# Attention pass of a graph kernel: transposed one-hots made by TensorE transposes and ScalarE copies instead of broadcast target rows

## Chip, cores and metric

One NeuronCore of a Trainium2 (trn2) chip runs one program. The metric is device time in microseconds (us), lower is better. "The time" of a kernel is the median of several runs; next to it stands one profiled execution, from which all rows of the profile come.

## What is computed

Two blocks, each a graph layer followed by a mixture-of-experts layer, on 6250 nodes of 256 features. The change touches the first graph layer alone, a graph attention layer over 206,250 edges that are sorted by target:

```
x = x + L0_gnn(layernorm(x))
h     = (x @ W).reshape(N, 4, 64)
a_src = einsum('nhc,hc->nh', h, att_src);  a_dst = einsum('nhc,hc->nh', h, att_dst)
e     = leaky_relu(a_src[src] + a_dst[dst], 0.2)
p     = exp(e - m[dst]);  denom = segment_sum(p, dst)
out   = segment_sum(p / denom[dst] * h[src], dst) + bias;  relu(out)
...
x = x + L0_ffn(...)    # 8 experts, 2 per node
x = x + L1_gnn(...)    # the same sorted edges, weighted sums, no attention
x = x + L1_ffn(...)    # a second attention over 131,072 unsorted edges, 4 experts
```

## The kernel before, in words

The sorted edges are cut into NS = 1664 tiles of 128 edges such that all targets of a tile lie in one block of 128 nodes. `plan_steps` (L451) makes, once, per tile the source of each edge, its target relative to the block's first node, its weight, and the block's number. `graph_pass` (L612) runs twice: with attention (tag g0, `attend` true; L745, L835, L877 to L901, L932 to L953, L977, L991 are its lines) and without (tag g1; L758, L846, L855, L991). Lines L855 and L991 are shared by both passes.

The tiles go in SG = 208 groups of GRP = 8, and the groups in rounds of RINGS = 4: gathered rows G and one-hots S have four slots, one for each group of a round. Below, "step k" is the work of one group. In the attention pass each engine runs its own instruction queue:

- GpSimd (POOL) issues eight indirect DMAs per group (L745), each fetching 128 source rows of 260 floats into G. Group k may start when all eight sums of group k-4 are done (L742); a small copy (L736) stages the indices first.
- SyncE (SP) issues, per group, one DMA (L723) that broadcasts 1024 relative targets to all 128 partitions, into a slot of ST; it waits until the spread of the group four before has used that slot (L722). The rows come from `target_rows`, a table in DRAM that `plan_steps` writes at L494 after a subtraction (L544).
- ScalarE (ACT) turns the broadcast rows into transposed one-hots in place with two activations over 128x1024: |row - lane| (L932) and relu(1 - that) (L934). It also makes the exponentials (L952, L953), and in the middle 200 groups a side job, a counting sort of the last layer's edges (L938, L942).
- TensorE (PE) first does the second half of the sums of group k-1 (four tiles, L991), then `spread` of group k+1 (L977): eight products of a transposed one-hot with the block's attention terms, which give each edge its target's term; then the first half of the sums of group k. A sum multiplies one-hot S by rows G into one of four PSUM banks (pM); a bank is used again when VectorE has added it (L990).
- VectorE (DVE), per step k: loads eight block numbers into registers (L447), waits for the spread of k (L875) and for the gather (L876), adds (L877, L878), leaky relu (L882), adds bank 0 of group k-1 into the accumulator (L855), subtracts (L888), makes all eight one-hots of group k+1 in one instruction (L835), adds banks 1 to 3, waits for the exponentials, and then alternates four multiplications of G by the factors (L899) with the last four adds.

The side job has three stretches: step 0 to 3 prepares, steps 4 to 103 count, steps 104 to 203 rank. In the rank stretch VectorE also does, every second step, a scan (L812, behind the one-hots) and a predicated copy (L818, at the end of the step).

The one instruction for eight one-hots reads the lane numbers from PSUM (pN, filled at L912):

```
v.tensor_tensor(S[:, r], pN[:, :].unsqueeze(1).broadcast_to([P, GRP, P]),
                REL[:, bass.ds(k * GRP, GRP)].unsqueeze(2).broadcast_to([P, GRP, P]),
                ALU.is_equal).then_inc(s["onehot"], 1)
```

The second pass makes them one at a time from SBUF, in turn with the adds (L846, `step_weighted`, L904). The last layer's slot pass has broadcast rows of its own (`slot_rows`), and is not touched.

Of the kernel before, what the change touches and what calls it, by code (L numbers as in the profile page):

```python
# [33 lines left out]
P = 128  # L34
# [145 lines left out]
def setup(sh, x):  # L180
# [9 lines left out]
    sh.minus_lane = sh.sb("minus_lane", [P, 1])  # L190
    s_x, s_cst, s_pre = sh.sem("x_loaded"), sh.sem("constants"), sh.sem("memsets")
    sh.x_ready = (s_x, 7 * 16)
    with Scope(nc) as sc:
# [3 lines left out]
        def _(pool):  # L197
# [6 lines left out]
            for out, mult in ((sh.lane, 1), (sh.minus_lane, -1)):  # L204
                pool.iota(out[:, :], [[0, 1]], base=0, channel_multiplier=mult,
                          allow_small_or_imprecise_dtypes=True).then_inc(s_cst, 1)
# [244 lines left out]
def plan_steps(sh, first_dst, edges, planned, planned_block, target_rows, stats):  # L451
# [9 lines left out]
                                          "stored", "relative")}  # L461
# [5 lines left out]
    with Scope(nc) as sc:  # L467
# [9 lines left out]
        FIRST = sc.sb("plan_FIRST", [P, SCH])  # L477
        T = sc.sb("plan_T", [P, SCH], I32)
        BI = sc.sb("plan_BI", [P, NS], I32)
# [11 lines left out]
        def _(sp):  # L491
            sp.dma_start(F[:, :], bcast_rows(first_dst[0, :])).then_inc(s["first"], 16)
            sp.wait_ge(s["relative"], NBK)
            sp.dma_start(target_rows.rearrange("(c p) m -> p c m", p=P), RF[:, 1, :, :]).then_inc(s["stored"], 16)  # L494
# [4 lines left out]
            sp.wait_ge(s["stored"], 16 * (NA + 2))  # L499
# [14 lines left out]
        def _(v):  # L514
# [16 lines left out]
            then(v.tensor_scalar(FIRST[:, :], TF[:, :], -1.0, float(P), ALU.add, ALU.mult))  # L531
# [3 lines left out]
            then(v.tensor_scalar(BI[:, :].rearrange("p (a b) -> p a b", a=4), flat, -1.0, None, ALU.add))  # L535
            norm.on_vector(v)
            for bk in range(NBK):
# [3 lines left out]
                for a in range(2):  # L541
                    v.tensor_copy(RF[:, a, c0:c1, :], RAW[:, a, c0:c1, :]).then_inc(s["float"], 1)
                v.wait_ge(s["float"], bk * 2 + 2)
                v.tensor_tensor(RF[:, 1, c0:c1, :], RF[:, 1, c0:c1, :], FIRST[:, c0:c1].unsqueeze(2).broadcast_to([P, c1 - c0, P]),  # L544
                                ALU.subtract).then_inc(s["relative"], 1)
                for a in range(NA):
                    v.wait_ge(s["turned"], bk * NA + a + 1)
                    out = pT[(bk * NA + a) % 2][:, 0:(c1 - c0) * P]
                    if a == 0:
                        v.tensor_copy(OSRC[:, cols], out).then_inc(s["out"], 1)  # L550
                    else:
                        v.tensor_copy(OUT[:, a - 1, cols], out).then_inc(s["out"], 1)
# [4 lines left out]
        def _(pe):  # L557
# [5 lines left out]
            for bk in range(NBK):  # L563
                for a in range(NA):
# [3 lines left out]
                    if a == 0:  # L568
                        pe.wait_ge(s["float"], bk * 2 + 1)
                    elif a == 1:  # L570
                        pe.wait_ge(s["relative"], bk + 1)
# [40 lines left out]
def graph_pass(sh, tag, planned, planned_block, table, width, acc, acc_zeroed, gather_done, rounds0, keep=None, gmax=None,  # L612
               sort=None, target_rows=None, place=0):
# [13 lines left out]
    if attend:  # L627
        names += ["iota", "far", "turned", "ad", "z", "lr", "arg", "p", "pcol", "gp"]
# [3 lines left out]
    s_rows = [sh.sem(f"{tag}_rows{r}") for r in range(RINGS)] if attend else None  # L632
    with Scope(nc) as sc:
# [18 lines left out]
        if attend:  # L652
            ST = sc.sb(f"{tag}_ST", [P, RINGS, GRP, P])
# [3 lines left out]
            pN = sc.ps(f"{tag}_pN", [P, P])  # L657
            pAX = [sc.ps(f"{tag}_pA{j}", [P, 512]) for j in range(2)]
            pA = [x[:, 0:GRP * HEADS].rearrange("p (u h) -> p u h", u=GRP) for x in pAX]
            pF = sc.ps(f"{tag}_pF", [P, 512])  # L660
            before, totals = pAX[0][:, 128:128 + NB + 1], pAX[0][:, 256:256 + NB + 1]
# [47 lines left out]
        def _(sp):  # L709
# [16 lines left out]
            if attend:  # L726
                over_groups(sp, rows)
# [1855 lines left out]
```

## Time and profile before

| what | value |
|---|---|
| time, median of 3 runs | 9814.81 us (9797.74 to 9833.64) |
| the profiled execution | 9757.08 us, span 9755.1 us |
| mean granted TensorE clock | 0.708 of 2.4 GHz |
| attention pass (first gather issue to last sum) | 205 to 3262 us |
| second graph pass | 4834 to 7507 us |

How to read the rows: times are us from the span's start, except means, which are ns. PE is TensorE's matmuls, PEld its weight loads, DVE VectorE, ACT ScalarE, POOL GpSimd, SPq the DMA issues of SyncE. An fp32 matmul stands as two PE records. In a group of instructions, "idle before" is the time that the engine stood idle right before instructions of the group, with what ended it: an instruction of another engine, a DMA, "issue" (nothing that the profile shows was waited for) or "remote" (a semaphore whose setter the profile does not tie to a record).

### The profile page before, as it was taken

Reading aid. Unit: us, or ns where it says so; the run is one execution under the profiler, and the core shown is the slowest. Engines: PE = TensorE matmul, PEld = TensorE weight load, DVE = VectorE, ACT = ScalarE, POOL = GpSimd, SP = SyncE. Lnnn points to the kernel's source line nnn. Section 1 sums busy time; section 2 is a strip of 40 time slices with the busy share of each in tenths; the row PEclk is TensorE's granted clock in tenths of the full one; section 3 lists DMA queues with packets and bytes.
Section 4 is the critical chain, followed back from the end, with each engine's and each line's share of the span. In section 5 each row is a group of like instructions: output and inputs, shape, how many; then the busy total and the mean of one; then the engine's idle time right before and its main releaser. Section 6 shows DMA issues by size and latency. Waiting matters only on the chain. (4 is left out here: it accounts for less than half of the span.)

```text
span 9755.1 us, 110833 instructions
## 1 busy us (share of the span) xinstructions
PE 5735.5 (59%) x25980; PEld 4596.0 (47%) x25981; DVE 3970.9 (41%) x10089; ACT 1833.0 (19%) x3782; POOL 5610.6 (58%) x6058
## 2 busy tenths in 40 slices
PE   3666656555555248888144444444444459898984
PEld 2444444434444247777133322322322348888884
DVE  4555555555555640000444444444443432222225
ACT  1222222222222023333000000000000123333331
POOL 3555555555555546666666666666666346666662
PEclk7666676666666669999566666666666757888886
DMA  3333333333333314444333222222222022222256
GB/s 128 113 116 115 115 116 113 103 99 102 103 103 100 109 56 135 135 135 136 115 88 88 81 81 80 81 81 79 81 81 61 1 56 64 65 66 66 63 63 158
DMA packets 459979, 909.45 MB, mean 93 GB/s; under 512 B 133272, under 2 KB 272908, under 8 KB 459615
## 3 DMA queue, kind: packets, MB, share of 16 engines
q0 software_dynamic: 237808, 481.17, 20.3%
q1 hardware_dynamic: 222062, 427.12, 13.0%
q8 instruction: 33, 0.54, 0.0%
q14 instruction: 76, 0.61, 0.0%
HBM read 836.02 MB, written 71.83 MB: 93 GB/s over the span
## 5 line engine op out<-in xcount | busy, mean ns | idle before, releaser
L991 PE MATMUL g_pM<-g_G,g_S 128*128 128x260 f32 (+1 forms) x6656 | 2555.0, 536 | 2857.8 <-DVE acc L855 1374.7
L991 PEld LDWEIGHTS g_pM<-g_G,g_S 128*128 128x128 f32 x6656 | 1608.6, 262 | 3692.7 <-DVE acc L855 2142.8
L745 POOL DMA_INDIRECT g_G<-table,g_STG x1664 | 1626.3, 977 | 1377.1 <-PE g_pM L991 872.6
L758 POOL DMA_INDIRECT g_G<-table,g_IDX x1664 | 1583.6, 952 | 891.0 <-issue 471.2
L855 DVE TENSOR_TENSOR acc<-g_pM,acc 128x260 f32 (+1 forms) x3328 | 1412.3, 424 | 1356.9 <-remote 588.4
L1551 POOL DMA_INDIRECT q_G<-table,slot x1072 | 1040.1, 970 | 636.3 <-issue 288.3
L607 POOL DMA_INDIRECT slots<-sort_PAIR,sort_ADDR x1024 | 1024.0, 1000 | 523.0 <-issue 310.8
L846 DVE TENSOR_SCALAR g_S<-iota,g_REL,g_WT 128x128 f32<-128x128 f32 x1664 | 596.1, 359 | 454.5 <-issue 274.7
L1337 PE MATMUL q_pH<-ew_XT,ew_W 128*128 (+1 forms) x3136 | 563.2, 352 | 58.3 <-issue 29.4
L977 PEld LDWEIGHTS g_pA<-keep,g_ST 128*128 128x128 f32 x3328 | 520.1, 245 | 119.8 <-issue 118.0
L1211 ACT ACTIVATE f_XT<-f_pT 128x512 f32<-128x512 f32 x49 | 28.9, 597 | 2902.3 <-issue 2736.0
L899 DVE TENSOR_TENSOR g_G<-g_G,g_pF 128x512 f32<-128x512 f32 x832 | 563.3, 677 | 0.0
L1337 PEld LDWEIGHTS q_pH<-ew_XT,ew_W 128*128 128x128 f32 x3136 | 525.1, 259 | 77.3 <-ACT ew_GT L1356 40.2
L2244 PE MATMUL e_pH<-e_XT,e_W 128*128 128x128 f32 x3360 | 447.1, 297 | 168.2 <-ACT e_XT L2188 151.1
L977 PE MATMUL g_pA<-keep,g_ST 128*128 x3328 | 515.6, 287 | 49.5 <-issue 34.5
L2244 PEld LDWEIGHTS e_pH<-e_XT,e_W 128*128 128x128 f32 x3360 | 428.3, 210 | 208.1 <-ACT e_GT L2205 177.8
L877 DVE TENSOR_TENSOR g_Z<-g_G,g_pA 128x32 f32<-128x32 f32 x208 | 39.0, 187 | 1102.4 <-remote 1012.3
L952 ACT ACTIVATE g_pF<-g_ARG 128x32 f32<-128x32 f32 x208 | 41.8, 201 | 2283.3 <-DVE g_ARG L888 1974.3
L2222 DVE TENSOR_TENSOR e_Y<-e_pY,ew_B 128x256 f32<-128x256 f32 x105 | 44.6, 425 | 986.6 <-PE e_pY L2252 882.6
L1347 PE MATMUL q_pY<-ew_W,ew_GT 128*128 128x256 f32 x1568 | 440.1, 430 | 2.8 <-issue 2.6
L2252 PE MATMUL e_pY<-ew_W,e_GT 128*128 x1680 | 389.2, 384 | 8.9 <-issue 7.7
L2205 ACT ACTIVATE e_GT<-e_pH,ew_VT 128x128 f32<-128x128 f32 x840 | 239.6, 369 | 693.8 <-remote 407.2
(319 smaller groups left out, 6384.0 us busy)
## 6 DMA issues: line engine op xcount, KB each, us to landing
e_W<-in_L_ffn_W SPq DMA_DIRECT2D x210, 512.0 KB
g_ST<-target_rows SPq DMA_DIRECT2D x208, 512.0 KB
sort_PAIR<-slot_rows SPq DMA_DIRECT2D x66, 512.0 KB
g_G<-table,g_STG POOLq DMA_INDIRECT x1664
g_G<-table,g_IDX POOLq DMA_INDIRECT x1664
ys_all<-ew_Y SPq DMA_DIRECT2D x196, 128.0 KB
sm_Y<-ys_all SPq DMA_DIRECT2D x28, 896.0 KB, 10.3
q_ST<-slot_rows SPq DMA_DIRECT2D x34, 512.0 KB
```

The source lines that it names most:

```text
L607: pool.indirect_dma_start(self.slots, bass.IndirectOffsetOnAxis(ap=self.ADDR[:, t:t + 1].bitcast(U32), axis=0), self.PAIR[:, t, :], None). ...
L745: pool.indirect_dma_start(G[:, r, u, :], None, table, bass.IndirectOffsetOnAxis(ap=STG[:, r, u:u + 1].bitcast(U32), axis=0)).then_inc(gath ...
L758: pool.indirect_dma_start(G[:, r, u, :], None, table, bass.IndirectOffsetOnAxis(ap=IDX[:, k * GRP + u:k * GRP + u + 1].bitcast(U32), axis= ...
L846: v.tensor_scalar(S[:, r, u, :], sh.iota[:, :], rel, WT[:, bass.ds(j, 1)], ALU.is_equal, ALU.mult).then_inc(s["onehot"], 1)
L855: v.tensor_tensor(sums, pM[u % BANKS][:, 0:width], sums, ALU.add).then_inc(s["added"], 1)
L899: v.tensor_tensor(rows, rows, fac, ALU.mult).then_inc(s["gp"], 1)
L977: m = pe.matmul(pA[r % 2][:, u, :], ST[:, r, u, :], nodes, start=True, stop=True)
L991: pe.matmul(pM[u % BANKS][:, 0:width], S[:, r, u, :], G[:, r, u, :], start=True, stop=True).then_inc(s["sum"], 1)
L1337: m = pe.matmul(self.pH[e % n][:, c, :], self.W1[:, e, k, c * P:(c + 1) * P], self.XT[:, bass.ds(i, 1), k, :].rearrange("p a m -> p (a m)" ...
L1347: m = pe.matmul(self.pY[e % n][:, 0:D], self.GT[:, e % 2, c, :], self.W2[:, e, c, :], start=(c == 0), stop=(c == self.HC - 1))
L1551: pool.indirect_dma_start(G[:, r, u, :], None, table, bass.IndirectOffsetOnAxis(ap=node_of_slot[:, 2 * (k * GRP + u):2 * (k * GRP + u) + 1 ...
L2244: m = pe.matmul(pH[j % 2][:, c, :], W1[:, j, k, c * P:(c + 1) * P], XT[:, j % 2, k, :], start=(k == 0), stop=(k == KC - 1))
```

## The change

The transposed one-hots of the attention pass no longer come from broadcast rows.

- `plan_steps` no longer makes `target_rows`: the DMA L494 and the subtraction L544 go. Relative targets are computed at the end, when the turned rows are copied out (one operation in place of a copy), for which a float copy BF of the block numbers is made, one more VectorE instruction.
- SyncE's broadcasts L723, ScalarE's L932 and L934, and the PSUM copy of the lane numbers are gone. ST has one slot of eight tiles, not four.
- VectorE makes the one-hots of group k+1 one at a time (`tensor_scalar` is_equal, from the lane numbers in SBUF, as the second pass does, with one operation in place of two), spread over step k: tiles 0, 1 after L878; 2, 3 after L882; 4 to 7 each behind one add of the first four. The scan of the rank stretch moves in front of L882. The first add moves behind L888.
- TensorE turns the one-hots of group k+1 in two halves (`transposes`): tiles 0 to 3 at the start of step k, ahead of the sums of group k-1; tiles 4 to 7 behind these sums, ahead of the spread. The result is in PSUM (pT, two banks).
- ScalarE copies each half from PSUM to ST (`copy`, 128x512): the first half at the start of its step, ahead of the exponentials; the second behind L938, ahead of L942.
- The spread waits for each half's copy. TensorE's wait for VectorE's one-hots moves from the sums to the transposes. The two pA tiles share one PSUM bank, and TensorE's wait for the side job's `base` chain (L999) goes.

```diff
@@ plan_steps
-            sp.wait_ge(s["relative"], NBK)
-            sp.dma_start(target_rows.rearrange("(c p) m -> p c m", p=P), RF[:, 1, :, :]).then_inc(s["stored"], 16)
...
+            then(v.tensor_scalar(BF[:, :].rearrange("p (a b) -> p a b", a=4), flat, -1.0, None, ALU.add))
...
-                v.wait_ge(s["float"], bk * 2 + 2)
-                v.tensor_tensor(RF[:, 1, c0:c1, :], RF[:, 1, c0:c1, :], FIRST[:, c0:c1].unsqueeze(2).broadcast_to([P, c1 - c0, P]),
-                                ALU.subtract).then_inc(s["relative"], 1)
...
+                    elif a == 1:
+                        v.scalar_tensor_tensor(OUT[:, 0, cols], BF[:, cols], -float(P), out, ALU.mult,
+                                               ALU.add).then_inc(s["out"], 1)
@@ graph_pass, sync
-            def rows(rnd, r):
-
-                k = rnd * RINGS + r
-                at_least(sp, s["ad"], k - RINGS + 1)
-                sp.dma_start(ST[:, r].rearrange("p u m -> p (u m)"),
-                             bcast_rows(target_rows.rearrange("t m -> (t m)")[bass.ds(k * (GRP * P), GRP * P)])).then_inc(s_rows[r], 16)
@@ graph_pass, vector
-            def onehots(rnd, r):
...
+                if attend:
+                    v.tensor_scalar(S[:, r, u, :], sh.iota[:, :], rel, None, ALU.is_equal).then_inc(s["onehot"], 1)
...
+                def next_onehots(us):
+                    if not last(rnd, r):
+                        for u in us:
+                            onehot(*after(rnd, r), u)
...
+                next_onehots((0, 1))
+                if phase == "rank" and r % 2 == 1:
+                    scan_block(b, r // 2)
 
                 v.wait_ge(s["z"], k * 2 + 2)
...
-                if after_first:
-                    add(k - 1, 0, blk[0])
+                next_onehots((2, 3))
                 v.wait_ge(s["lr"], k + 1)
                 v.tensor_tensor(ARG[:, par], L[:, par, 0], L[:, par, 1], ALU.subtract).then_inc(s["arg"], 1)
-                if not last(rnd, r):
-                    onehots(*after(rnd, r))
-                if phase == "rank" and r % 2 == 1:
-                    scan_block(b, r // 2)
-                for u in range(1, HG):
+                for u in range(HG):
                     add_before(u)
+                    next_onehots((HG + u,))
@@ graph_pass, scalar
-                def turned_onehots(rnd, r):
...
+                def copy(k, hf):
+                    a.wait_ge(s["turned"], 2 * k + hf + 1)
+                    at_least(a, s["ad"], k)
+                    sl = slice(hf * HG, (hf + 1) * HG)
+                    a.activation(ST[:, sl, :], pT[:, sl, :], ACT.Copy).then_inc(s["copied"], 1)
@@ graph_pass, tensor
+            def transposes(k, r, hf):
+                at_least(pe, s["copied"], 2 * k - 1 + hf)
+                pe.wait_ge(s["onehot"], k * GRP + (hf + 1) * HG)
+                for u in range(hf * HG, (hf + 1) * HG):
+                    m = pe.transpose(pT[:, u, :], S[:, r, u, :], sh.ident[:, :])
+                m.then_inc(s["turned"], 1)
+
             def spread(k, r):
...
-                pe.wait_ge(s["turned"], k + 1)
                 for u in range(GRP):
+                    if u % HG == 0:
+                        pe.wait_ge(s["copied"], 2 * k + u // HG + 1)
...
             def step_attend(rnd, r, phase=None, b=None):
                 k = rnd * RINGS + r
+                if not last(rnd, r):
+                    transposes(k + 1, (r + 1) % RINGS, 0)
                 if not first(rnd, r):
                     sums(k - 1, (r - 1) % RINGS, range(HG, GRP))
                 if not last(rnd, r):
+                    transposes(k + 1, (r + 1) % RINGS, 1)
                     spread(k + 1, (r + 1) % RINGS)
                 sums(k, r, range(HG))
```

## Rows read from the trace of the kernel before

**Rows 1.** The page: busy time, share of the span and instructions of each engine.
```profile
PE 5735.5 (59%) x25980; PEld 4596.0 (47%) x25981; DVE 3970.9 (41%) x10089; ACT 1833.0 (19%) x3782; POOL 5610.6 (58%) x6058
```
**Rows 2.** Both graph passes: span, busy PE, PEld, DVE, ACT, POOL, clock, DMA share, GB/s.
```profile
205.00:3262.00 3057.00, 1763.36 (x6640) 1307.43 (x6641) 1655.86 (x3636) 757.62 (x1083) 1667.71 (x1870) 0.66 0.37 108
4834.00:7507.00 2673.00, 1246.38 (x3328) 800.07 (x3328) 1156.16 (x3328) 0.00 (x0) 1746.01 (x1828) 0.66 0.29 82
```
**Rows 3.** Costliest groups of instructions, attention pass: count, busy us, mean ns, idle before.
```profile
L745 POOL DMA_INDIRECT g_G<-table,g_STG x1664 | 1626.3, 977 | 1377.1 <-PE g_pM L991 872.6 <-issue 490.2 <-remote 11.2
...
L835 DVE TENSOR_TENSOR g_S<-g_pN,X 128x1024 f32<-128x1024 f32 x207 | 252.1, 1218 | 0.0
L934 ACT ACTIVATE g_ST<-g_ST,ones 128x1024 f32<-128x1024 f32 x208 | 238.8, 1148 | 6.8
L932 ACT ACTIVATE g_ST<-g_ST,minus_lane 128x1024 f32<-128x1024 f32 x208 | 236.4, 1137 | 24.0 <-DMA g_ST<-target_rows 23.2
...
L812 DVE TENSOR_TENSOR_SCAN X<-ones,g_BASE,X 128x1024 f32<-128x1024 f32 x50 | 117.1, 2342 | 0.0
...
L818 DVE COPY_PREDICATED X<-X 128x1024 f32<-128x1024 int32 x50 | 67.1, 1343 | 0.0
```
**Rows 4.** VectorE's L877, once a step: first 100 steps counted, then 100 ranking.
```profile
L877 DVE TENSOR_TENSOR g_Z<-g_G,g_pA x100: 186/189/190, 283.0 to 1649.9; 128x32 f32<-128x32 f32 x100
...
  remote: 463.1, 35
...
L877 DVE TENSOR_TENSOR g_Z<-g_G,g_pA x100: 160/189/204, 1675.5 to 3218.2; 128x32 f32<-128x32 f32 x100
...
  remote: 536.5, 47
```
**Rows 5.** Timeline of VectorE, one step: start us, us, instruction [idle before].
```profile
1005.78 0.19 DVE L877 TENSOR_TENSOR g_Z<-g_G,g_pA 128x32 f32<-128x32 f32 x1 [14.86 <-remote]
...
1009.22 0.43 DVE L855 TENSOR_TENSOR acc<-g_pM,acc 128x260 f32 x1 [0.21 <-DVE acc L855]
...
1013.76 0.19 DVE L877 TENSOR_TENSOR g_Z<-g_G,g_pA 128x32 f32<-128x32 f32 x1 [0.38 <-issue]
```
**Rows 6.** Timeline of TensorE around the same step.
```profile
988.56 1.94 PE L977 MATMUL g_pA<-keep,g_ST 128*128 x16 [0.61 <-issue]
990.36 3.33 PE L991 MATMUL g_pM<-g_G,g_S 128*128 128x260 f32 x8
1006.86 1.23 PE L991 MATMUL g_pM<-g_G,g_S 128*128 128x260 f32 x2 [13.17 <-DVE acc L855]
...
1011.19 1.93 PE L977 MATMUL g_pA<-keep,g_ST 128*128 x16
```
**Rows 7.** Timeline of GpSimd: end of a run of 16 gathers, start of the next.
```profile
1001.82 0.94 POOL L745 DMA_INDIRECT g_G<-table,g_STG  x1 [0.30 <-issue]
...
1012.21 0.97 POOL L745 DMA_INDIRECT g_G<-table,g_STG  x1 [9.24 <-PE g_pM L991]
```
**Rows 8.** The granted clock (third number from the end) in two short stretches.
```profile
1005.00:1011.00 6.00, 3.81 (x8) 2.29 (x8) 4.71 (x12) 3.84 (x7) 0.00 (x0) 0.50 0.28 87
1011.50:1014.00 2.50, 2.50 (x20) 2.38 (x20) 2.12 (x7) 0.47 (x1) 1.49 (x2) 1.00 0.07 12
```
**Rows 9.** VectorE in the second pass: one-hots and adds in turn.
```profile
6043.67 0.34 DVE L846 TENSOR_SCALAR g_S<-iota,g_REL,g_WT 128x128 f32<-128x128 f32 x1
6043.96 0.42 DVE L855 TENSOR_TENSOR acc<-g_pM,acc 128x256 f32 x1
```
**Rows 10.** Four fp32 transposes of a projection; ScalarE copies of 128x512 from PSUM.
```profile
123.88 1.09 PE L422 MATMUL p_pT<-ident,p_XR 128*128 128x128 f32 x4 [17.13 <-DVE p_XR L353]
...
L1211 ACT ACTIVATE f_XT<-f_pT x49: 579/597/599, 7517.7 to 7772.8; 128x512 f32<-128x512 f32 x49
```
**Rows 11.** Costliest groups of instructions, second pass.
```profile
L758 POOL DMA_INDIRECT g_G<-table,g_IDX x1664 | 1583.6, 952 | 891.0 <-issue 471.2 <-remote 198.3 <-PE g_pM L991 190.8
...
L846 DVE TENSOR_SCALAR g_S<-iota,g_REL,g_WT 128x128 f32<-128x128 f32 x1664 | 596.1, 359 | 454.5 <-issue 274.7 <-PE g_pM L991 97.0 <-DVE acc L855 36.1
```

More of the change, by code:

```diff
@@ L203, in _ @@
                       allow_small_or_imprecise_dtypes=True).then_inc(s_cst, 1)
-            for out, mult in ((sh.lane, 1), (sh.minus_lane, -1)):
-                pool.iota(out[:, :], [[0, 1]], base=0, channel_multiplier=mult,
-                          allow_small_or_imprecise_dtypes=True).then_inc(s_cst, 1)
+            pool.iota(sh.lane[:, :], [[0, 1]], base=0, channel_multiplier=1,
+                      allow_small_or_imprecise_dtypes=True).then_inc(s_cst, 1)
             pool.wait_ge(s_pre, 4)
@@ L627, in graph_pass @@
     if attend:
-        names += ["iota", "far", "turned", "ad", "z", "lr", "arg", "p", "pcol", "gp"]
+        names += ["turned", "copied", "ad", "z", "lr", "arg", "p", "pcol", "gp"]
     if ranking:
@@ L656, in graph_pass @@
             ARG = sc.sb(f"{tag}_ARG", [P, 2, GRP, HEADS])
-            pN = sc.ps(f"{tag}_pN", [P, P])
-            pAX = [sc.ps(f"{tag}_pA{j}", [P, 512]) for j in range(2)]
-            pA = [x[:, 0:GRP * HEADS].rearrange("p (u h) -> p u h", u=GRP) for x in pAX]
+            pT = sc.ps(f"{tag}_pT", [P, GRP, P])
+            pAX = sc.ps(f"{tag}_pA", [P, 512])
+            pA = pAX[:, 0:2 * GRP * HEADS].rearrange("p (a u h) -> p a u h", a=2, u=GRP)
             pF = sc.ps(f"{tag}_pF", [P, 512])
-            before, totals = pAX[0][:, 128:128 + NB + 1], pAX[0][:, 256:256 + NB + 1]
+            before, totals = pAX[:, 128:128 + NB + 1], pAX[:, 256:256 + NB + 1]
         block = sc.block()
@@ L845, in onehot @@
                     at_least(v, s["sum"], (rnd * RINGS + r - RINGS + 1) * GRP)
-                v.tensor_scalar(S[:, r, u, :], sh.iota[:, :], rel, WT[:, bass.ds(j, 1)],
-                                ALU.is_equal, ALU.mult).then_inc(s["onehot"], 1)
+                if attend:
+                    v.tensor_scalar(S[:, r, u, :], sh.iota[:, :], rel, None, ALU.is_equal).then_inc(s["onehot"], 1)
+                else:
+                    v.tensor_scalar(S[:, r, u, :], sh.iota[:, :], rel, WT[:, bass.ds(j, 1)],
+                                    ALU.is_equal, ALU.mult).then_inc(s["onehot"], 1)
             def add(k, u, blk):
@@ L909, in step_weighted @@
                     add(rnd * RINGS + r, u, blk[u])
+            for u in range(GRP):
+                onehot(0, 0, u)
             if attend:
-                v.tensor_copy(pN[:, :], sh.iota[:, :]).then_inc(s["iota"], 1)
-                v.wait_ge(s["iota"], 1)
-                onehots(0, 0)
                 over_groups_sorting(v, step_attend, bases, addresses)
@@ L919, in _ @@
             else:
-                for u in range(GRP):
-                    onehot(0, 0, u)
                 over_groups(v, step_weighted)
@@ L948, in step @@
                     if not last(rnd, r):
-                        turned_onehots(rnd + (r + 1) // RINGS, (r + 1) % RINGS)
+                        copy(k + 1, 0)
                     a.wait_ge(s["arg"], k + 1)
@@ L960, in step @@
                         distances(n, b, r // 2)
+                    if not last(rnd, r):
+                        copy(k + 1, 1)
+                    if sorting:
                         equal(n, b, r // 2, phase == "count")
-                turned_onehots(0, 0)
+                copy(0, 0)
+                copy(0, 1)
                 over_groups_sorting(a, step)
@@ L998, in prefix @@
                 pe.matmul(totals, sh.ones[:, :], CNT[:, :], start=True, stop=True).then_inc(s["prefix"], 1)
-                pe.wait_ge(s["base"], 7)
             def step_attend(rnd, r, phase=None, b=None):
                 k = rnd * RINGS + r
+                if not last(rnd, r):
+                    transposes(k + 1, (r + 1) % RINGS, 0)
                 if not first(rnd, r):
@@ L1014, in _ @@
             if attend:
+                transposes(0, 0, 0)
+                transposes(0, 0, 1)
                 spread(0, 0)
```

47 lines of the change are left out of this document (14 added, 33 removed).

## Prediction, made before the changed kernel was run

> **What bounds the kernel now.** The page first [rows 1]: no engine is busy above 59%, so waits set the time. The change is all in the first graph pass (the set-up ahead of it apart), so that pass is read alone [rows 2]: 3057 us for 208 steps, 14.7 us a step, TensorE 58% busy, VectorE 54%, ScalarE 25%, GpSimd 55%, DMA engines 37%, no one of them near its limit.
>
> The groups of instructions [rows 3] give the floor that GpSimd sets: eight gathers of 0.98 us with 0.30 us between them [rows 7] and a small copy, 10.3 us a step. The floor that VectorE sets is read from one step that meets no wait [rows 5]: from one L877 to the next 7.98 us. Both are far below 14.7.
>
> The rest is in the waits of L877 [rows 4]. In the counting stretch (1675.5 - 283.0) / 100 = 13.9 us a step, and 35 waits called "remote" sum to 463 us, 13.2 us each; in the ranking stretch (3218.2 - 1675.5) / 99 = 15.6 us a step, and 47 such waits, 11.4 us each. So 82 long waits, 1000 us in all, are a third of the pass. One of them is in [rows 5, 6, 7]: L877 starts at 1005.78 after 14.86 us of nothing, though the spread that it needs is on TensorE's record from 988.56 to 990.50. GpSimd ran gathers back to back until 1002.76, and 3.0 us later everything moves at once. TensorE sums, and 6.4 us after L877 the slot is free for the next gather (1012.21). I read this as a loop: release, 6 us of sums, a run of gathers in whose later part TensorE's signals don't get through, release. What holds the signals the trace doesn't say, and I treat it as given.
>
> What does a longer step cost in such a loop? The side job answers: in the ranking stretch VectorE has (2.34 + 1.34) / 2 = 1.84 us more work per step [rows 3], and the step is 15.6 - 13.9 = 1.7 us longer. Slope 0.92: nearly every microsecond put into the chain between two L877s comes out as time, although VectorE is half idle.
>
> **The change, part by part.**
>
> *VectorE.* Out goes L835, 1.22 us [rows 3]. In come eight one-hots. In the second pass such a one-hot takes the engine for 0.29 us until the add behind it starts [rows 9]. Four stand between the small operations, 4 x 0.29 = 1.16 us. The other four stand behind adds, which today leave 0.21 us idle each, waiting for the add before [rows 5], so that a pair needs about what the add alone needs; 0.3 us is left for all four. Sum: -1.2 + 1.2 + 0.3 = +0.3 us. Bounds: nothing, and 8 x 0.29 - 1.22 = +1.1 us where no gap is filled. Taken: 8.3 us for VectorE's step.
>
> *TensorE.* In come eight transposes. The nearest row is four in 1.09 us [rows 10]; at the other clock level perhaps half, 0.55 us. The path to the next L877 is now: fourth one-hot ready at 1.6 us (L877, L878 and L882 0.6, four one-hots 1.2, less an overlap), four transposes, four sums of the group before, four transposes, a copy, the spread's second half. At 1.2 GHz: 1.6 + 1.1 + 3.3 (eight records, [rows 6]) + 1.1 + 0.6 + 1.9 = 9.6 us. At 2.4 GHz the sums are paced by the adds, the fourth of which ends near 4.3 us: 4.3 + 0.4 + 0.55 + 0.6 + 1.0 (half of the 1.93 us of sixteen records [rows 6]) = 6.9 us. Today the spread is done at 1011.19 + 1.93 - 1005.78 = 7.3 us. In the step shown the clock was 0.50 up to 1011 and 1.00 while the spread ran [rows 8], so one such step has some of either. Time from L877 to L877: between 8.3 (VectorE) and 9.6 us; I take the middle, 9.0, that is +1.0 us over 7.98.
>
> *ScalarE.* Out go 1.14 + 1.15 us a step [rows 3], in come two copies of 0.60 us [rows 10]. The engine is 25% busy, so the 1.1 us saved are worth nothing. But its queue has a new order: the first copy stands ahead of the exponentials and waits for the first four transposes, at 2.7 us. The factors are then ready at 3.1 us, and VectorE needs them behind its fourth add, at 4.3 us: hidden with 1.2 us to spare. The second copy stands ahead of L942, whose result the scan of the next step awaits, and the scan now stands nearer the start of its step. At 9.6 us after L877 L942 is just done; I put 0.3 us on 50 steps, 15 us, with 0 and 60 us as ends.
>
> *SyncE and DMA.* 208 broadcasts go with their waits; each had four slots of lead, and ScalarE waited for one in the whole pass, the first, 23 us [rows 3], beside the first gather. Cost and gain 0 by themselves; whether their traffic feeds the long waits is a rival below.
>
> *Release of GpSimd.* The sums of the group before now follow the first transposes, so the slot comes free 0 to 1.1 us later than 6.4 us after L877. It is part of the same loop and in the slope, not added again.
>
> *The wait for the `base` chain* (L999) happens once in the pass and hides nothing else: 0.
>
> *The set-up.* One operation over 1664 columns more, four subtractions and one store fewer, once. By the pace of L818 (1.34 us for 1024 columns [rows 3]) some 2 us each way; taken as 0, ends -5 and +5.
>
> **The sum.** 0.92 x 1.0 us x 207 = 190 us, and 15 for the scan: +205 us. Against the profiled execution's 9757 us that makes 9962; the median of the runs, 9814.8, is 58 us above the profiled time, and on it I get 10020 us. Bounds of the known terms: 0.92 x 0.3 x 207 = +57, and 0.92 x 1.6 x 207 + 60 + 5 = +370.
>
> **Does the one-hot block the gathers?** The second pass runs these one-hots beside its gathers, and there a gather issue takes 952 ns, against 977 ns in the attention pass, which has none [rows 2, 3, 11]. So nothing is added for it. The Trainium skill (SBUF — State Buffer, Who interferes with whom) says that a `tensor_scalar` with its operands in SBUF can take the port pair that GpSimd needs for writing descriptors; the row doesn't show it as longer issues.
>
> **Rivals.**
>
> 1. *The one-hots hold up the gathers after all.* Eight of 0.34 us [rows 9] are 2.7 us a step. Under GpSimd's 10.3 us that would be 13, still below 14.7, but each long wait ends only behind its run of gathers, so 82 waits grow by 2.7 to 5.4 us: +220 to +440 on the sum, about 10350 us. This is what the Trainium skill's rule would make of it. Against: the 952 ns. Chance 0.07.
>
> 2. *A long wait in nearly every step.* If the path over TensorE and ScalarE passes GpSimd's 10.3 us, the next gather run always meets an unfinished step. From 9.6 us that is not far. Price: today 82 waits of 12.2 us; 36 more are +440 us, 10255 us. For it: the ranking stretch has 47 where the counting one has 35. Against: at the upper clock the path is 6.9 us. Chance 0.13.
>
> 3. *Faster: the long waits shrink with the broadcasts gone.* 512 KB a step leave the DMA queues, and the second pass, which has no broadcasts, needs 2673 / 208 = 12.9 us a step [rows 2]. If a third of the 1000 us of waits went, -333 + 205 = -128 us, 9687 us. If all did, the step would be GpSimd's 10.3 us, some 900 us less. Against: in the long wait shown SyncE had issued nothing, since its issue hangs on the same spread. It decides from 205 us on, 20% of the waits. Chance 0.25.
>
> 4. *No change that can be told.* The new work falls into the long waits, and the loop's length is set by the gather runs. "Tell" means 0.3%, 29 us. Against: the slope of 0.92. Chance 0.09.
>
> The forecast itself, +57 to +370 us, has 0.46.
>
> **The numbers.** Predicted time 10020 us, the likeliest case. Its own range is 9870 to 10185. The range for 8 in 10 goes on into rival 3 to its one-third price, 9690, which leaves out about half of that rival, and up to 10330, past rival 2, which leaves out most of rival 1 and some of rival 2: 0.12 and 0.08 outside. Faster by over 0.3%: 0.25. Within 0.3%: 0.09. Slower: 0.46 + 0.13 + 0.07 = 0.66.
>
> **What the changed profile would show.** If I am right: the distance of two L877s without a wait is 8.3 to 9.6 us, ended by TensorE's spread when the clock is 0.50; the number of "remote" waits is 82 or somewhat more; steps of 14.9 us counting and 16.6 ranking; transposes near 1.1 us for four; copies of 0.60 us; gather issues still near 0.95 us; ScalarE's waits for L888 shorter, since it now waits for the transposes. Rival 1 shows as gather issues above 1.2 us. Rival 2 shows as over 110 long waits. Rival 3 shows as the sum of the "remote" waits well below 1000 us. I am wrong if the step without a wait is as long as before, or if the sum of long waits moves by more than 200 us either way.

## The result, and the profile after

The changed kernel takes 9618.4, 9656.7 and 9731.0 us, and 14563.5 us in a fourth, disturbed execution that is left out of the ratio; the kernel before, beside it, takes 9824.2 us (median). The ratio is 0.9844, 95% interval 0.9817 to 0.9871. That is 1.6% faster, where +205 us had been forecast: the sign is wrong. The median of all four executions, 9693.9 us, is at the lower edge of the predicted range (9690), that of the three, 9656.7 us, below it. The profiled execution is the fastest one and spans 9616.5 us against 9755.1. The page, as in [rows 1]:

```profile
PE 5882.3 (61%) x27644; PEld 4830.0 (50%) x27645; DVE 4091.1 (43%) x11540; ACT 1580.0 (16%) x3782; POOL 5636.3 (59%) x6057
```

Both passes, columns as in [rows 2] (span, busy PE, PEld, DVE, ACT, POOL, granted clock, DMA share, GB/s):

```profile
213.00:3105.00 2892.00, 1913.81 (x8309) 1530.57 (x8309) 1764.65 (x5092) 507.30 (x1083) 1700.45 (x1870) 0.74 0.29 77
4680.00:7360.00 2680.00, 1229.81 (x3302) 791.86 (x3303) 1152.81 (x3308) 0.00 (x0) 1745.78 (x1828) 0.67 0.29 82
```

TensorE and VectorE do more than before, ScalarE less, and the attention pass is 3057 - 2892 = 165 us shorter; the second pass stands. The groups of the attention pass that answer to [rows 3]:

```profile
L728 POOL DMA_INDIRECT g_G<-table,g_STG x1664 | 1653.2, 994 | 1172.9 <-issue 493.0 <-PE g_pM L979 466.5 <-remote 211.0
...
L881 DVE TENSOR_TENSOR g_G<-g_G,g_pF 128x512 f32<-128x512 f32 x830 | 562.6, 678 | 168.2 <-ACT g_pF L929 134.5 <-issue 33.1
...
L822 DVE TENSOR_SCALAR g_S<-iota,X 128x128 f32<-128x128 f32 x1659 | 446.6, 294 | 8.4 <-issue 6.8 <-DVE acc L833 0.9
L955 PE MATMUL g_pT<-ident,g_S 128*128 128x128 f32 x1664 | 326.9, 331 | 517.2 <-DVE g_S L822 487.6 <-issue 29.1
...
L911 ACT ACTIVATE g_ST<-g_pT 128x512 f32<-128x512 f32 x416 | 248.0, 596 | 2401.3 <-PE g_pT L955 1502.8 <-remote 725.0 <-issue 173.2
```

L860 is what L877 was, VectorE's first operation of a step. It answers to [rows 4], first the counting stretch, then the ranking one:

```profile
L860 DVE TENSOR_TENSOR g_Z<-g_G,g_pA x101: 186/189/190, 292.3 to 1595.4; 128x32 f32<-128x32 f32 x101
...
  remote: 80.9, 6
  PE g_pA L966: 35.9, 51
...
L860 DVE TENSOR_TENSOR g_Z<-g_G,g_pA x103: 160/188/220, 1603.7 to 3100.7; 128x32 f32<-128x32 f32 x103
...
  remote: 433.3, 42
```

So (1595.4 - 292.3) / 100 = 13.0 us a step against 13.9, and (3100.7 - 1603.7) / 102 = 14.7 against 15.6. The long waits went from 82 to 48, from 1000 to 514 us, 382 us of this in the counting stretch.

The pass got only 165 us shorter, not 486, because the steps between the long waits became longer. Of 100 counting steps before, 59 are shorter than 11.5 us (9.6 us in the mean) and 31 longer than 20 us. After, 67 lie between 11.5 and 13.5 us, which is about GpSimd's eight gathers and a pause, and 7 are longer than 20 us. Steps in which VectorE waits for nothing have become rare. Here is one, as [rows 5], on VectorE:

```profile
884.07 0.19 DVE L860 TENSOR_TENSOR g_Z<-g_G,g_pA 128x32 f32<-128x32 f32 x1 [11.11 <-PE g_pM L979]
...
884.28 0.47 DVE L822 TENSOR_SCALAR g_S<-iota,X 128x128 f32<-128x128 f32 x2
...
885.30 0.42 DVE L833 TENSOR_TENSOR acc<-g_pM,acc 128x260 f32 x1
885.63 0.28 DVE L822 TENSOR_SCALAR g_S<-iota,X 128x128 f32<-128x128 f32 x1
885.93 0.43 DVE L833 TENSOR_TENSOR acc<-g_pM,acc 128x260 f32 x1
...
891.93 0.19 DVE L860 TENSOR_TENSOR g_Z<-g_G,g_pA 128x32 f32<-128x32 f32 x1 [0.36 <-issue]
```

and on TensorE, as [rows 6]; the granted clock from 884.1 to 892.0 was 1.00:

```profile
885.33 0.65 PE L955 MATMUL g_pT<-ident,g_S 128*128 128x128 f32 x4 [2.30 <-DVE g_S L822]
885.82 2.58 PE L979 MATMUL g_pM<-g_G,g_S 128*128 128x260 f32 x8
888.24 0.60 PE L955 MATMUL g_pT<-ident,g_S 128*128 128x128 f32 x4
889.10 1.94 PE L966 MATMUL g_pA<-keep,g_ST 128*128 x16 [0.27 <-issue]
```

891.93 - 884.07 = 7.86 us: with all the added work the step without a wait is 0.1 us shorter than before. It is not the clock that does this: the other three such steps of the counting stretch, at a mean clock of 0.78, take 7.84 to 7.85 us. The spread is done at 891.04, 0.9 us ahead of its use.

What changed is GpSimd. In the trace of before its gathers often come as two groups of eight with nothing between, a run of 16; this is the stretch ahead of [rows 7]:

```profile
970.62 0.97 POOL L745 DMA_INDIRECT g_G<-table,g_STG  x1 [5.18 <-PE g_pM L991]
...
982.90 0.97 POOL L745 DMA_INDIRECT g_G<-table,g_STG  x1 [2.33 <-PE g_pM L991]
...
993.02 0.97 POOL L745 DMA_INDIRECT g_G<-table,g_STG  x1 [0.16 <-issue]
```

The slot for the group at 993.02 was free by then, so GpSimd stopped for 0.16 us only, and VectorE got the spread that was ready at 990.50 at 1005.78, behind the whole run of 16 [rows 5, 6]. After the change:

```profile
1003.79 0.97 POOL L728 DMA_INDIRECT g_G<-table,g_STG  x1 [2.54 <-remote]
...
1016.31 0.97 POOL L728 DMA_INDIRECT g_G<-table,g_STG  x1 [2.45 <-PE g_pM L979]
...
1029.97 0.97 POOL L728 DMA_INDIRECT g_G<-table,g_STG  x1 [2.15 <-remote]
...
1042.31 0.97 POOL L728 DMA_INDIRECT g_G<-table,g_STG  x1 [2.39 <-remote]
```

Eight gathers, a pause of 2.2 to 2.5 us, eight gathers: the signals that stood still get through in each pause. Counted over the pass in both traces (a run ends where more than 1.6 us lie between two gathers), there are 72 runs of 16 and 36 of 8 before, 38 and 99 after; the rest are mostly of 15, 7 and 1.

The pauses became more, but not more time. From the last gather of a group to the first of the next there are 956 us before, summed over the pass, and 755 us after; 83 of these gaps were above 6 us before, 42 are after. GpSimd's gathers themselves take 28 us more. That makes 201 - 28 = 173 us, and the pass is 3043 - 2875 = 168 us shorter from the first to the last of these VectorE operations.

### The profile page after: what moved, and what is told of

It is laid out like the page before. It is cut to its first block and busy times, and to the rows that moved or that the text cites. A ratio compares the mean times of both kernels' runs of the same rounds, so it can differ in the third digit from the quotient of the medians.

```text
span 9616.5 us, 116917 instructions
## 1 busy us (share of the span) xinstructions
PE 5882.3 (61%) x27644; PEld 4830.0 (50%) x27645; DVE 4091.1 (43%) x11540; ACT 1580.0 (16%) x3782; POOL 5636.3 (59%) x6057
## 2 busy tenths in 40 slices
DMA packets 428348, 799.55 MB, mean 83 GB/s; under 512 B 129927, under 2 KB 267899, under 8 KB 427982
## 5 line engine op out<-in xcount | busy, mean ns | idle before, releaser
L979 PE MATMUL g_pM<-g_G,g_S 128*128 128x260 f32 (+1 forms) x6656 | 2451.1, 521 | 1683.9 <-issue 666.8
L728 POOL DMA_INDIRECT g_G<-table,g_STG x1664 | 1653.2, 994 | 1172.9 <-issue 493.0
L955 PE MATMUL g_pT<-ident,g_S 128*128 128x128 f32 x1664 | 326.9, 331 | 517.2 <-DVE g_S L822 487.6
L911 ACT ACTIVATE g_ST<-g_pT 128x512 f32<-128x512 f32 x416 | 248.0, 596 | 2401.3 <-PE g_pT L955 1502.8
L881 DVE TENSOR_TENSOR g_G<-g_G,g_pF 128x512 f32<-128x512 f32 x832 | 563.9, 678 | 168.2 <-ACT g_pF L929 134.5
L955 PEld LDWEIGHTS g_pT<-ident,g_S 128*128 128x128 f32 x1664 | 255.5, 174 | 634.8 <-DVE g_S L822 494.4
L822 DVE TENSOR_SCALAR g_S<-iota,X 128x128 f32<-128x128 f32 x1664 | 448.3, 295 | 18.3 <-DMA X<-in_fsrc_t 9.9
```

Of the source, the lines that this page charges most:

```text
L728: pool.indirect_dma_start(G[:, r, u, :], None, table, bass.IndirectOffsetOnAxis(ap=STG[:, r, u:u + 1].bitcast(U32), axis=0)).then_inc(gath ...
L881: v.tensor_tensor(rows, rows, fac, ALU.mult).then_inc(s["gp"], 1)
L955: m = pe.transpose(pT[:, u, :], S[:, r, u, :], sh.ident[:, :])
L979: pe.matmul(pM[u % BANKS][:, 0:width], S[:, r, u, :], G[:, r, u, :], start=True, stop=True).then_inc(s["sum"], 1)
```

## Theories

**P, the pauses.** In the later part of a run of gathers TensorE's signals don't get through, mostly until 2 to 3 us after its end. What a run of 16 costs is then a freeze of some 13 us. In the old kernel the next release often gets through in the early part of a run, so that GpSimd goes on behind its eighth gather without a stop. In the new one TensorE transposes before it does the sums that free the slot; the release falls later in the step, more often isn't through when the eighth gather is issued, and the run ends there.

**T, the traffic** (the prediction's rival 3): the broadcasts fed the waits.

**R**: it is the later release, with fewer groups ahead, and not the pause. And a last one: **the unloading** of ScalarE, the higher clock (0.74 against 0.66) or VectorE's new order does it.

What the traces of before and after say of P: all 73 waits of L877 above 8 us in before follow a spread that ended inside a run of 15 gathers or more. The sum that frees the next slot ends 7.0 us into the run before (median of 114 such places), and 81 of these releases get through; after, it ends 8.0 us into the run (126 places), and 40 get through. From the eighth group on, after has 97 gaps of 1.5 to 3.5 us between groups; in 76 of them the freeing sum had ended before the run did, and the next gather starts 4.5 us behind that sum (median), where it takes 0.8 us when no gathers are in the way. What lets one release through and holds another is not told by its time alone: of those that fall 6 to 9 us into a run in before, 64 get through and 33 don't. That stays open.

## The experiments

The kernels were measured in three series, each on one chip with the kernel before beside them, and all ratios are to that kernel in the same series. Its own median was 9663, 9805 and 9799 us in the three, so microseconds are compared inside a series only: in the first even the stretch behind the last gather of the second pass, which no kernel here touches, was 2209 to 2226 us, in the other traces 2259 to 2270. "Pass" is from the first to the last L877 (L860) in the trace; steps are means of a stretch without its first ones; "pauses" is the time between the last gather of a group and the first of the next, summed over the pass; runs are counted as above.

| kernel (series) | ratio, 95% interval | pass us | steps counting, ranking | pauses us | runs of 16 / of 8 |
|---|---|---|---|---|---|
| before | 1 | 3043 | 13.8, 15.6 | 956 | 72 / 36 |
| after | 0.9844 (0.9817 to 0.9871) | 2875 | 13.0, 14.7 | 755 | 38 / 99 |
| traffic (1) | 0.9787 (0.9744 to 0.9830) | 2823 | 12.8, 14.4 | 701 | 42 / 92 |
| quiet (1) | 1.0008 (0.9998 to 1.0019) | 3054 | 14.2, 15.4 | 968 | 73 / 23 |
| late_b (1) | 0.9557 (0.9541 to 0.9572) | 2606 | 12.4, 12.7 | 504 | 3 / 160 |
| late_a (1) | 0.9651 (0.9635 to 0.9668) | 2678 | 12.6, 13.3 | 522 | 1 / 185 |
| landed (2) | 0.9594 (0.9562 to 0.9626) | 2674 | 12.6, 13.3 | 561 | 0 / 191 |
| onehots (2) | 0.9903 (0.9858 to 0.9948) | 3075 | 14.0, 15.6 | 992 | 73 / 28 |
| exp_first (2) | 0.9774 (0.9727 to 0.9821) | 2820 | 12.9, 14.2 | 702 | 32 / 108 |
| sums_first (2) | 1.0035 (1.0015 to 1.0055) | 3103 | 14.4, 15.5 | 997 | 34 / 105 |
| late_both (3) | 0.9562 (0.9528 to 0.9595) | 2664 | 12.6, 13.1 | 544 | 2 / 180 |
| late8 (3) | 0.9989 (0.9972 to 1.0006) | 3041 | 13.9, 15.5 | 953 | 75 / 36 |
| late_exp (3) | 0.9686 (0.9655 to 0.9718) | 2763 | 13.1, 13.6 | 623 | 0 / 188 |
| landed_a (3) | 0.9591 (0.9559 to 0.9623) | 2664 | 12.5, 13.2 | 546 | 0 / 191 |

**Does the traffic matter?** Two kernels, one from each side.

*traffic*, the changed kernel with this added to SyncE (ScalarE waits for the row semaphore as it did before):

```diff
+            def rows(rnd, r):
+                k = rnd * RINGS + r
+                at_least(sp, s["ad"], k - RINGS + 1)
+                sp.dma_start(SPARE[:, r].rearrange("p u m -> p (u m)"),
+                             bcast_rows(planned[2].rearrange("t m -> (t m)")[bass.ds(k * (GRP * P), GRP * P)])).then_inc(s_rows[r], 16)
```

> The changed kernel with the 208 broadcasts of 512 KB put back, at the old kernel's pace, into a buffer that nobody reads (their source is the planned weights, as the target rows are no longer stored). Theory P (pacing): the gain comes from GpSimd's gather runs, which the later release of the slots cuts from 16 gathers to 8 with a pause between; the traffic has no part in it. Expected 9665 to 9740 us, attention pass about 2890 us, few waits above 10 us in the counting stretch. Theory T (traffic, rival 3 of the prediction): the long waits shrank since the broadcasts left the queues. Then they come back, and the added work on the path stays: 9900 us or more, over 60 waits above 8 us.

*quiet*, the kernel before with one broadcast for all steps:

```diff
-                             bcast_rows(target_rows.rearrange("t m -> (t m)")[bass.ds(k * (GRP * P), GRP * P)])).then_inc(s_rows[r], 16)
+                             bcast_rows(target_rows.rearrange("t m -> (t m)")[0:GRP * P])).then_inc(s_rows[r], 16)
...
-                over_groups(sp, rows)
+                rows(0, 0)
...
-                    a.activation(ST[:, r], ST[:, r], ACT.Abs, bias=sh.minus_lane[:, 0:1]).then_inc(s["far"], 1)
+                    a.activation(ST[:, r], FIXED[:, :, :], ACT.Abs, bias=sh.minus_lane[:, 0:1]).then_inc(s["far"], 1)
```

> The kernel before with a single broadcast instead of 208; ScalarE turns the same rows each step, so the one-hots' transposes are wrong for all groups but one, with the same instructions on ScalarE, VectorE and TensorE. Theory P: 9780 to 9850 us, the same 22/8/11 us pattern of steps and 80 or so remote waits summing to 900 to 1050 us. Theory T: the whole gain and more (nothing has been added to the path): 9600 us or less, remote waits under 700 us.

(It goes to a buffer of its own, FIXED.) With the traffic back the gain stays (and the ratio is a little better than the change's own and than either theory had; the two intervals just overlap), without it there is none. The pages' DMA rows show that the traffic really changed. First of after, then of traffic, then of quiet:

```profile
DMA packets 428348, 799.55 MB, mean 83 GB/s; under 512 B 129927, under 2 KB 267899, under 8 KB 427982
```
```profile
DMA packets 458300, 908.62 MB, mean 96 GB/s; under 512 B 133255, under 2 KB 271227, under 8 KB 457934
```
```profile
DMA packets 430170, 800.90 MB, mean 83 GB/s; under 512 B 129959, under 2 KB 269595, under 8 KB 429806
```

Theory T falls, and with it the unloading of the queues as a reason of any kind.

**Does the place of the release matter?** *late_b* is the kernel before with one number changed in GpSimd's wait, *late_a* is the changed kernel with the same edit:

```diff
-                at_least(pool, s["sum"], (k - RINGS + 1) * GRP)
+                at_least(pool, s["sum"], (k - RINGS + 1) * GRP + HG)
```

> The kernel before with one number changed: GpSimd waits for four sums more (the first half of the next group) before it gathers into a slot, about 3 to 4 us later in each step. Theory P: the gather runs of 16 are cut into 8 and 8, the long waits shrink, and the kernel gets faster though it releases its slots later: 9600 to 9740 us. Theory T: nothing of the traffic changes, a later release can only cost: 9815 to 9950 us.

> The changed kernel with the same later release. Theory P: its runs are already of 8; the pause grows from 2.4 us to 4 us or so, the remaining long waits of the ranking stretch (42 of 10 us) go down; 9550 to 9700 us. Theory T: no slack is gained, 9700 to 9850 us.

One number in the old kernel, which only makes GpSimd wait longer, is worth 4.4%, nearly three times the whole change. GpSimd in late_b, three groups in a row:

```profile
1012.56 0.97 POOL L745 DMA_INDIRECT g_G<-table,g_STG  x1 [2.37 <-remote]
...
1024.94 0.97 POOL L745 DMA_INDIRECT g_G<-table,g_STG  x1 [2.45 <-PE g_pM L991]
...
1037.24 0.97 POOL L745 DMA_INDIRECT g_G<-table,g_STG  x1 [2.37 <-remote]
```

Its step is now the run and the pause: 12.3 us from one group to the next. The expectations were given for a kernel before of 9815 us; on that scale late_b is 9380 us and late_a 9472, both below the ranges of theory P, so the theory had the sign and undersized the gain. Theory T had neither.

*late8* goes further the same way: `+ GRP` instead of `+ HG`, a whole group later.

> The kernel before with GpSimd waiting for all eight sums of the next group, not four, so that at most three groups are ahead. If the pause alone matters and three groups are enough to hide the landing of the gathers: 0.955 to 0.965, as late_b. If the release is now too late, so that the steps wait for the gathers: above 0.97.

The ratio is in the second branch, but its reason is wrong. L877 hardly waits for gathers; the old pattern is back:

```profile
L877 DVE TENSOR_TENSOR g_Z<-g_G,g_pA x208: 163/188/225, 224.8 to 3265.5; 128x32 f32<-128x32 f32 x104
...
  remote: 960.1, 84
...
  DMA g_G<-table,g_STG: 16.0, 2
```

84 remote waits of 960 us in the whole pass (84 and 1012 in before, counted in the same way), 75 runs of 16. A whole group later is the same place in the step, one step on, and the pairing is back. So it is not lateness that helps late_b.

**Does the pause alone do it?** *landed* leaves the releases of before as they are and makes the pause with GpSimd's own gathers:

```diff
                 at_least(pool, s["sum"], (k - RINGS + 1) * GRP)
+                at_least(pool, gather_done[(r - 1) % RINGS], (rnd + (r > 0) + rounds0) * 16 * GRP)
```

> The kernel before with one wait more: GpSimd starts the gathers of a group only when those of the group before have landed, so that each run of 8 ends with a pause, whatever TensorE and VectorE do; the slots are released as before. Theory P: the pause is what counts. Steps of 12.3 to 13 us, no runs of 16, 0.955 to 0.965 of the time before. Theory R (it is the later release as such, with fewer groups ahead, and not the pause): 0.99 to 1.01.

```profile
1014.74 0.97 POOL L746 DMA_INDIRECT g_G<-table,g_STG  x1 [2.44 <-issue]
...
1027.09 0.97 POOL L746 DMA_INDIRECT g_G<-table,g_STG  x1 [2.42 <-DMA g_G<-table,g_STG]
```

The step is 12.35 us, the pause 2.4, and the waits of VectorE have another cause (here L878 is the step's first operation):

```profile
L878 DVE TENSOR_TENSOR g_Z<-g_G,g_pA x208: 186/188/190, 224.6 to 2898.5; 128x32 f32<-128x32 f32 x104
...
  DMA g_G<-table,g_STG: 743.5, 167
  remote: 179.8, 38
```

Where 82 waits for signals had summed to 1000 us, 38 are left with 180 us; VectorE waits for the gathers themselves. That is theory P in its plainest form: GpSimd issues the same 1664 gathers, stops after every eighth on purpose, and the kernel is 4.1% faster. With late8 (later release, the old pattern, no gain) and landed (a pause behind each group, no later release, the gain) theory R falls. Landed doesn't part a pause in the issuing from fewer gathers in flight, since it makes both.

The granted clock isn't the reason either. It is 0.66 in the pass of before and 0.74 in that of after, but late_b and landed, which gain most, have 0.65 and 0.64.

**Which part of the change makes the pause?** *exp_first* moves ScalarE's first copy behind the two exponentials. *sums_first* has that too, and TensorE's old place for the sums:

```diff
-                if not last(rnd, r):
-                    transposes(k + 1, (r + 1) % RINGS, 0)
                 if not first(rnd, r):
                     sums(k - 1, (r - 1) % RINGS, range(HG, GRP))
                 if not last(rnd, r):
+                    transposes(k + 1, (r + 1) % RINGS, 0)
                     transposes(k + 1, (r + 1) % RINGS, 1)
```

> The changed kernel with ScalarE's first copy moved behind the exponentials, so that the factors don't wait for the transposes. The path to the multiplications gets shorter, the spread at most 0.5 us later. Theory P: the slots are freed as late as in the changed kernel; 0.975 to 0.986 of the time before. If the wait for the exponentials was the price of the change, up to 1 us a step is gained: 0.965.

> As exp_first, and TensorE does the four sums of the group before ahead of all eight transposes, so the slot is released as early as in the kernel before. Theory P: the runs of 16 come back, 60 or more of them, and with them the added work shows: 0.995 to 1.02 of the time before. If the gain came from anything else in the change (less on ScalarE, a higher clock, no broadcasts): 0.975 to 0.985, as exp_first.

The two differ in the order of eight TensorE instructions, and 2.6 points lie between them, more than the change's whole gain. All else of the change is in sums_first: lighter ScalarE, no broadcasts, one-hots one at a time. So it is TensorE's order. But the count of runs doesn't show it: the expected 60 runs of 16 did not come, there are 34, and exp_first has 32. What parts the two is the sum of the pauses, 997 us against 702: sums_first has 74 pauses of 3.5 to 6 us, exp_first 7. In the counting stretch the release meets the run in another way. One step there, on VectorE:

```profile
851.42 0.42 DVE L833 TENSOR_TENSOR acc<-g_pM,acc 128x260 f32 x1
...
854.29 0.43 DVE L833 TENSOR_TENSOR acc<-g_pM,acc 128x260 f32 x1 [2.25 <-PE g_pM L979]
...
857.86 0.43 DVE L833 TENSOR_TENSOR acc<-g_pM,acc 128x260 f32 x1 [2.95 <-remote]
```

and on GpSimd:

```profile
855.74 0.94 POOL L728 DMA_INDIRECT g_G<-table,g_STG  x1 [0.30 <-issue]
...
861.26 0.97 POOL L728 DMA_INDIRECT g_G<-table,g_STG  x1 [4.38 <-PE g_pM L979]
```

Sums and adds hand each other a bank, one at a time, and here they do it in the later part of a run: two handovers take 2.3 and 3.0 us of waiting, and the pause grows to 4.4 us. By the traces it is the same kind of freeze, which hits elsewhere. Runs of 16 are thus one way to lose, not the only one.

*onehots*, the kernel before with VectorE's part alone:

```diff
-                if not last(rnd, r):
-                    onehots(*after(rnd, r))
...
+                next_onehots((0, 1))
...
+                next_onehots((2, 3))
...
+                for u in range(HG):
+                    add_before(u)
+                    next_onehots((HG + u,))
```

> The kernel before with only VectorE's part of the change: eight one-hots from SBUF one at a time between its other work, the scan moved up, in place of the one instruction; broadcasts, ScalarE and TensorE's order stay. Theory P with TensorE's order as the cause: the slots are released nearly as early as before, the runs of 16 stay: 0.995 to 1.01 of the time before. If VectorE's new order makes the pause by itself, 0.98 to 0.985 as for the whole change. If the prediction's price for this part holds: +57 us, 1.006.

Inconclusive. Its executions spread from 9621 to 9815 us, and the profiled one (9815) was the slowest, so its 73 runs of 16 don't show where the faster ones gain. 0.9903 lies between the branches; the prediction's +57 us for this part, 1.006, is outside the interval.

**What does the added work cost, where the pauses are alike?** Two more kernels: *landed_a* is the changed kernel with landed's wait, *late_exp* is late_a with exp_first's order.

> The changed kernel with the pause of landed (a group's gathers start when those of the group before have landed). By theory P the length of a step is GpSimd's 10.3 us and 2.1 us of pause in both kernels, and the added work hides in the counting stretch: 12.4 us a step there, with up to 1 us more in the ranking stretch: 0.958 to 0.967 of the time before. If the added work is on the path as the prediction had it (0.9 us a step): 0.975 or more.

> The changed kernel with the later release (late_a, 0.965) and with the exponentials ahead of ScalarE's first copy (exp_first). With paced runs the added work shows by itself: late_a stands 0.9 points above late_b. If the wait for the exponentials makes most of that, 0.955 to 0.959; if the transposes and one-hots do, 0.963 to 0.967.

landed_a against landed: 0.9591 against 0.9594, nothing, with each interval 0.3 points to a side. late_a against late_b: +0.94 points, 92 us; of the 72 us by which the passes differ, some 60 are in the ranking stretch (100 steps of 13.3 us against 12.7). Most of this is paid by GpSimd: its 800 gather issues there take 1081 ns in the mean against 1020, 49 us in all. sums_first against before, with the sums at their old place in both but pauses that aren't the same: +0.35 points, 34 us. So the price is 0 to 92 us by what stands around it. late_exp brought nothing over late_a, and its 0.9686 is in neither branch, though its interval reaches the second; whether the exponentials' wait costs something (exp_first is 0.7 points below after, and the intervals touch) stays open.

**Does it carry over?** *late_both* has late_b's edit in the second pass too.

> late_b with the same later release in the second pass too, which today has mostly runs of 16 gathers and 12.9 us a step. Theory P (pauses): its steps come down to the 12.4 us that late_b and landed show in the attention pass, 90 to 110 us less: 0.943 to 0.950 of the time before. If the second pass is bound by something other than held signals, or pays for the pause what it gains by it: 0.955 to 0.960, as late_b.

It doesn't: 0.9562 against late_b's 0.9557. In its second pass the groups still come in pairs, with 101 pauses of over 3 us (4.8 in the median) at 207 places, 102 (4.6) in late_b; between the two groups of a pair stands at most one other issue of GpSimd (L607). So the later release doesn't part the pairs there, and this kernel doesn't test what pauses would bring in that pass. Landed's wait was not tried there.

late_b, late_both, landed and landed_a are the fastest, not told apart, and beat both kernels: 0.956 to 0.959.

## Why the prediction was wrong

**The step that failed first: "I treat it as given".** The prediction read the loop rightly (release, sums, a run of gathers in which signals don't get through, release), and that 82 such waits make 1000 us. It then kept their number fixed and put a price only on what was added between them. But the change moved the release inside that loop, and the waits were what moved: 1000 to 514 us. Under *Release of GpSimd* the text had the very cause, "the slot comes free 0 to 1.1 us later", and booked it as a small cost, "part of the same loop and in the slope". It was the gain. What the views of before could have shown was the pairing: 72 runs of 16 next to 36 of 8, and all 73 waits above 8 us at runs of 15 or more.

Both of its own tests say so: "I am wrong if the step without a wait is as long as before, or if the sum of long waits moves by more than 200 us"; the step is 7.86 against 7.98 us, the sum moved by 486.

**The slope of 0.92.** It came from comparing the ranking with the counting stretch, where the scan adds 1.84 us. It held for the scan; it isn't a property of the loop. One microsecond in the right place (late_b) had a slope far below zero.

**TensorE's path, "between 8.3 and 9.6 us; I take the middle, 9.0".** Measured 7.86 us at the upper clock, where the text's own figure for that clock was 6.9 (the spread is done 6.97 us after L860) and VectorE's time was the longer one. At a mixture of both levels, the case that the middle was meant for, it was 7.84 to 7.85 us, so TensorE's path didn't set the length there either. In most other counting steps GpSimd's gathers and pause do. The term of 190 us is 0 in the wait-free steps, and by the pairs above 0 to 92 us in all, against +205 forecast.

**VectorE, 8.3 us.** 7.86: "A pair needs about what the add alone needs" was right: two adds with a one-hot between start 885.93 - 885.30 = 0.63 us apart, 0.64 before (1009.22 and the add ahead of it). The other four took 2 x 0.47 us, not 1.16, and in exchange 1.22 us went.

**ScalarE, 0 with 1.2 us to spare.** Not quite: L881 waits 134.5 us for the exponentials. In the wait-free step the margin is there: they are through 2.8 us after L860, and L881 starts at 3.7. In other steps the first copy waits for a held signal of the transposes, and the exponentials stand behind it in the queue. In the step that starts at 1007.73 the transposes end at 1010.94, the copy starts at 1015.35 and the first exponential at 1015.84. The text priced the new order at the undisturbed times only. What the order costs stays open, as said at late_exp, and no run measured the 15 us for the scan by itself.

**Right:** copies of 0.60 us (596 ns); the broadcasts cost and gave nothing (quiet, traffic); transposes 0.60 to 0.65 us for four at the upper clock, estimated at 0.55. Rival 1 didn't occur at its price: a gather issue takes 994 ns beside one-hots, 977 before, 17 x 1664 = 28 us in all. These means hide two stretches, though. Counting, it is 951 ns before and 955 after; ranking, 1005 and 1032, and the text's comparison of 977 with 952 in the second pass took no note of that. Ranking, before and after (shortest, median, longest in ns):

```profile
L745 POOL DMA_INDIRECT g_G<-table,g_STG x792: 943/949/2200, 1681.6 to 3214.7; - x198
```
```profile
L728 POOL DMA_INDIRECT g_G<-table,g_STG x807: 942/949/2986, 1603.3 to 3085.5; - x162
```

The longest gather issues run beside the scan, which after the change has one-hots right before and behind it. The Trainium skill (SBUF — State Buffer, Who interferes with whom) says that a `tensor_scalar` can take the port pair that VectorE shares with GpSimd and block it; this trace shows some 4 ns a gather of it where the one-hots stand without the scan. Rival 2, more long waits, went the other way (its price, 10255 us, also left out the +205 of the sum). Rival 3 had the right symptom, shorter long waits, with the chance of 0.25 and a price (one third gone: 9687 us) near the outcome, but the cause it named was the traffic, and that was wrong.

## What to carry to other kernels

Where engines wait on each other in a ring, and one of them issues long runs of gathers, look at the length of its runs and at what waits until they end, before pricing any instruction. A change that adds work can gain by moving a release, and one that saves work can lose by it. A deliberate pause, or a release in the middle of the step, is a one-line thing to try, and where it helps it may be worth more than the change under study.

## What was not expected of the hardware

- Signals of TensorE to VectorE, GpSimd and ScalarE can stand still in the later part of a run of gathers and arrive mostly 2 to 3 us after its end: ready at 990.50, seen at 1005.78 with a run of 16 that ended at 1002.76. The runs that were cut to 8 have pauses of 2.2 to 2.5 us, and in 76 of 97 the release was ready before the run's end. Whether it is the issuing engine or the gathers' packets that hold them up, no run here tells.
- 512 KB of broadcasts a step (908.62 - 799.55 = 109 MB in all) changed neither these waits nor the time (1.0008).
- A gather issue of 0.95 us took 2.20 us beside VectorE's scan of 2.34 us (before, at 1714.68), and 2.99 us beside the scan with one-hots around it (after, at 1604.53).
- Standing still on purpose made GpSimd, the busiest engine of the pass after TensorE, finish earlier: 1664 gathers from 212.9 to 2893.5 us in landed, to 3256.4 us in late8.
